# A wavelet convolution and a similarity filter: channel-major partitions, fewer and wider transfers, residual sums in another order

## The chip, the cores and the metric

The kernel runs on one core of a Trainium2 chip. The metric is the device time of one execution in microseconds (us). TensorE (PE) multiplies matrices, VectorE (DVE) and ScalarE (ACT) do elementwise work, GpSimd (POOL) and SyncE (SP) here mostly start DMA transfers, each on a queue of its own.

## The reference

The input x is 8 images of 32 channels, 128 x 128, float32. `_gn` normalises each channel of each image over its pixels. Two layers follow, each with a residual:

```python
x = x + _L0_conv_ref(_gn(x), w0, w1, w2, bias)   # three Haar levels; on each a 5x5 convolution 128 -> 128 channels
x = x + _L1_conv_ref(_gn(x), spatial_weight)

# _L1_conv_ref, K = 5
patches = _extract_patches(x)                             # 25 shifted copies of x
dot = einsum('bchw,bckhw->bkhw', x, patches)
sim = dot / maximum(norm_x[:, None] * norm_p, 1e-8)
weight = (sim + 1.0) * 0.5 * spatial_weight[None, :, None, None]
out = einsum('bckhw,bkhw->bchw', patches, weight)
```

A Haar level splits an image into the four pixels of each 2x2 cell (the quadrants, q = 0 to 3), mixes them, convolves at half size and mixes back. So 32 channels times 4 quadrants fill the 128 partitions.

## The kernel before

Partition 32q + c holds quadrant q of channel c. The first layer convolves image i while the second layer filters image b = i - 1; `iteration(i, ...)` of each engine is one such pair, and the engines meet through counting semaphores, in an order that is written out by hand. Iteration 0 has only the first layer, iterations 1 to 7 have both, and the last has only the second.

An iteration has a head and eight tiles. In the head PE sums the low-pass images and convolves levels 1 and 2, and the first three half-bands of image b are prepared. Tile j (`CONV_TILES` is 8) is point j of a Winograd form of the level-0 convolution (`conv_points`), and between its matmuls, at the places in `HOOKS`, stands the filter work of unit j. A unit is a half-band: 16 rows by 32 columns of each quadrant, with a border, so `UN` = 612 pixels a partition, or `FN` = 720 when it is cut into four overlapping strips.

Half-band h is prepared three tiles ahead of its use (`AHEAD`):
- ACT writes it to st_x2 (`half_in`) and squares it; PE sums the squares over the channels (`norm_piece`, two pieces into stat_ps); ACT takes roots and squared norms (`norms`, into st_a and st_n). Before it writes st_n, ACT waits until the stores of half-band h - 2 have landed (`half_saved`).
- DVE refines the root and makes unit vectors (`units_open`, `units_refine`, `units_close`); ACT and DVE split vectors and values in a high and a low float16 part (st_hl, st_v).
- SP stores all this to HBM (`save_half`): five transfers, to d_hl, d_v (two each) and d_n.
- SP loads it again in another layout (`load_unit`): eleven transfers into unit_mem, that is keys (two), queries (four), values (one) and norms (four, each of 72 rows of 40 bytes). `load_unit(b, u + 2)` stands behind `save_half(b, u + 3)` in SP's queue.

The filter of unit u on PE: `unit_here` waits for the loads; `gram` multiplies keys and queries, DVE turns each product into weights (`weights`, L1012, 128 x 512), `key_values` transposes values, `filter_group` (L1375) multiplies values and weights into out_ps, 32 output columns for each of four row groups g, which are four groups of columns of the array. `residual` (L1364) adds x1 into the same bank: 16 float32 products with 32 columns of a scaled identity as weights, which the hardware runs as 32 instructions. Its loops run over g outside and q inside. ACT writes the result to ostage (`result`), SP to HBM (`store_band`).

POOL's queue loads the raw image twice into `ring`, and reads the outputs of levels 2 and 1 back from HBM into `up`, always in four transfers of 32 partitions, one for each quadrant.

Of the kernel before, what the change touches and what calls it, by code (L numbers as in the profile page):

```python
# [28 lines left out]
P = 128  # L29
# [49 lines left out]
SAVES, LOADS = 80, 176  # L79
# [4 lines left out]
PAD_EDGE = P * (SH + SW - 1)  # L84
# [21 lines left out]
def host_constants():  # L106
# [4 lines left out]
    for c in range(C):  # L111
        for t in range(Q):
            for q in range(Q):
                mix[4 * c + t, C * q + c] = 0.5 * haar[t, q]
                gather[C * q + c, t, C * t + c] = 0.5
    part = np.arange(P)
    average = np.where(part[:, None] % C == part[None] % C, 0.25, 0).astype(np.float32)
    same_quadrant = (part[:, None] // C == part[None] // C).astype(np.float32)
# [37 lines left out]
def build(nc, x, w0, w1, w2, bias, spatial, square, gather, tapmask, unpair, out):  # L156
    ctx = ExitStack()
    with ctx:
# [27 lines left out]
        st_n = sb("st_n", [P, 2, UN], F32)  # L186
# [29 lines left out]
        ones_row = sq_c[0:1, 2, 0:C]  # L216
# [29 lines left out]
        d_n = dram("d_n", [B, 2 * BANDS, Q, UN], F32)  # L246
# [18 lines left out]
        wcomb = sem("wcomb")  # L265
        live_set, live_kept = sem("live_set"), sem("live_kept")
# [93 lines left out]
        def _(sp):  # L360
# [7 lines left out]
            for q in range(Q):  # L368
                sp.dma_start(small[C * q:C * q + C, 6:7], bias.rearrange("(c a) -> c a", a=1)).then_inc(const_in, 16)
# [7 lines left out]
            def save_half(b, h):  # L377

                sp.wait_ge(unit_low, START + 8 * b + h + 1)
                for hl in range(2):  # L380
                    sp.dma_start(d_hl[b, h, hl].rearrange("c q n -> q c n"), st_hl[:, hl, h % 2, :]).then_inc(half_saved[h % 2], 16)  # L381
                for hl in range(2):
                    sp.dma_start(d_v[b, h, hl].rearrange("c q n -> q c n"), st_v[:, hl, h % 2, :]).then_inc(half_saved[h % 2], 16)  # L383
                sp.dma_start(d_n[b, h], st_n[0:P:C, h % 2, :]).then_inc(half_saved[h % 2], 16)

            def load_unit(b, u):
# [19 lines left out]
                norms = d_n[b, u].rearrange("(a q) (h w) -> a (q h) w", a=1, w=SW)  # L406
                for e in range(GROUPS):
                    row = 64 + C * (e // 2)
                    sp.dma_start(norm_strips[s][row:row + 1, e % 2].rearrange("a (n w) -> a n w", w=KW),  # L409
                                 norms[:, :, TW * e:TW * e + KW]).then_inc(unit_in[s], 16)  # L410
# [31 lines left out]
        def _(pool):  # L442
# [5 lines left out]
            def load_raw(batch, c, slot):  # L448
                alone(pool)
                for q in range(Q):  # L450
                    cp = q % 2
                    src = x[batch].rearrange("c (h a) w -> c a h w", a=2)[:, q // 2, CHUNK * c:CHUNK * (c + 1), cp:IMG]
                    dst = ring[C * q:C * q + C, slot, :].rearrange("p (h w) -> p h w", w=IMG)[:, :, 0:IMG - cp]
# [19 lines left out]
            def load_up(i, n):  # L473
# [7 lines left out]
                src = d_z1[i, 2 * C * a:2 * C * (a + 1), BANK * half:BANK * (half + 1)].rearrange("(b c) n -> c b n", c=C)  # L481
                for q in range(Q):
                    pool.dma_start(up[C * q:C * q + C, :].rearrange("c (b n) -> c b n", b=2), src).then_inc(up_in, 16)  # L483

            def iteration(i, nxt, conv, ls):
                if conv:
# [7 lines left out]
                    for q in range(Q):  # L494
                        pool.dma_start(up[C * q:C * q + C, :].rearrange("c (q n) -> c q n", q=Q),
                                       d_z2[i].rearrange("(q c) n -> c q n", c=C)).then_inc(up2_in, 16)
# [27 lines left out]
        def _(act):  # L524
# [98 lines left out]
            def norms(b, h, p):  # L623
# [15 lines left out]
            def count_own(b, h):  # L639
# [3 lines left out]
                nc.scalar.activation(st_hl[:, 1, h % 2, 0:UN], st_n[:, h % 2, :], ACT.Sign, bias=edge[:, :], scale=-1.0,  # L643
# [112 lines left out]
        def _(dve):  # L756
# [17 lines left out]
            def set_live(i):  # L774
# [3 lines left out]
                V.tensor_copy(mean_ls, mean_conv).then_inc(live_set, 1)  # L778
# [168 lines left out]
            def units_open(b, h):  # L947
# [7 lines left out]
                ch.link(dve, V.scalar_tensor_tensor(out=st_b[:, :], in0=st_b[:, :], scalar=-0.5, in1=st_n[:, h % 2, :],  # L955
                                                    op0=ALU.mult, op1=ALU.mult))
# [32 lines left out]
            def set_flag(b, h):  # L989
# [3 lines left out]
                V.tensor_scalar(flag[:, h % FLAGS:h % FLAGS + 1], stat_ps[0:1, 0:1], 0.5, float(P * UN // 2 - pads), ALU.mult, ALU.add)\  # L993
                    .then_inc(flag_done, 1)

            def weights(b, u, k, short_ones):
# [9 lines left out]
                with dve.If(short_ones > 0):  # L1006

                    V.tensor_scalar(dst, guard_ps[0:KN, :].rearrange("p (t n) -> p t n", t=2), 1.0, None, ALU.min)
# [19 lines left out]
            def iteration(i, conv, ls):  # L1028
# [25 lines left out]
                if ls:  # L1054
                    for h in range(AHEAD):
                        units_open(b, h)
                        units_refine(h)
# [15 lines left out]
                for j in range(CONV_TILES):  # L1073
                    h = j + AHEAD
                    if ls:
                        dve.wait_ge(flag_done, START + 8 * b + j + 1)
                        alone(dve)
                        short_ones = dve.value_load(flag[0:1, j % FLAGS:j % FLAGS + 1], min_val=0, max_val=P * UN)
                    for k in range(PAIRS):
                        if ls:  # L1080
# [5 lines left out]
                            if h < 2 * BANDS:  # L1086
# [4 lines left out]
                                if k == 4:  # L1091
                                    units_refine(h)
# [134 lines left out]
        def _(pe):  # L1227
# [124 lines left out]
            def residual(b, u):  # L1352
# [8 lines left out]
                for g in range(BANDS):  # L1361
                    row = BH * r + TH * g
# [180 lines left out]
```

## Time and profile before

| | us |
|---|---|
| median of 3 runs | 2235.41 |
| lowest and highest | 2229.73, 2240.69 |
| the profiled execution, its own time | 2231.01 |
| its span in the trace | 2229.3 |
| PE busy | 1737.3 |
| DVE busy | 1363.9 |
| ACT busy | 742.9 |

The span is the stretch from the first to the last instruction. Busy times of different engines overlap. A granted clock of 1.00 is TensorE's full speed. Iterations 1 to 7 take about 251 to 257 us each and the last some 192 us.

### The profile page before, as it was taken

Reading aid. Unit: us, or ns where it says so; the run is one execution under the profiler, and the core shown is the slowest. Engines: PE = TensorE matmul, PEld = TensorE weight load, DVE = VectorE, ACT = ScalarE, POOL = GpSimd, SP = SyncE. Lnnn points to the kernel's source line nnn. Section 1 sums busy time; section 2 is a strip of 40 time slices with the busy share of each in tenths; the row PEclk is TensorE's granted clock in tenths of the full one; section 3 lists DMA queues with packets and bytes.
Section 4 is the critical chain, followed back from the end, with each engine's and each line's share of the span. In section 5 each row is a group of like instructions: output and inputs, shape, how many; then the busy total and the mean of one; then the engine's idle time right before and its main releaser. Section 6 shows DMA issues by size and latency. Waiting matters only on the chain.

```text
span 2229.3 us, 53057 instructions
## 1 busy us (share of the span) xinstructions
PE 1737.3 (78%) x19007; PEld 988.9 (44%) x19007; DVE 1363.9 (61%) x1995; ACT 742.9 (33%) x1318; POOL 430.6 (19%) x760
## 2 busy tenths in 40 slices
PE   5776887978878787878778787878779787876576
PEld 3542344545444444535345344545345444443354
DVE  6427756756677456856577456755578465865453
ACT  2320243423333243423333243423333252423341
POOL 1343322012311123012310123012300224010000
PEclk7888897889989898989989898999989898987577
DMA  5243337552666337562656447552754447571555
GB/s 164 75 106 95 85 104 174 151 137 78 187 155 159 94 104 191 153 140 78 179 156 151 97 114 196 152 139 79 176 149 128 117 105 201 127 174 38 141 145 127
DMA packets 128073, 296.57 MB, mean 133 GB/s; under 512 B 44532, under 2 KB 77300, under 8 KB 127220
## 3 DMA queue, kind: packets, MB, share of 16 engines
q1 hardware_dynamic: 90864, 190.39, 33.5%
q0 software_dynamic: 36864, 101.47, 17.6%
q8 instruction: 230, 3.77, 0.8%
q14 instruction: 115, 0.94, 0.1%
HBM read 221.92 MB, written 69.83 MB: 131 GB/s over the span
## 4 chain that ended last, share of the span: by engine, by line
PE 41%; DMA 17%; DVE 15%; SPq 13%; issue 10%; ACT 2%; DVEq 1%; POOL 1%; ACTq 0%; POOLq 0%
PE conv L1274 11%; DMA unit_mem<-d_n 8%; DMA d_n<-st_n 8%; PE conv L1248 6%; PE gram L1339 5%; PE out_ps L1364 5%; PE out_ps L1375 3%; SPq L409 3%; PE conv L1233 3%; PE stat_ps L1297 3%; SPq L383 3%; SPq L402 2%; SPq L381 2%; PE vals_ps L1322 2%; PE conv L1484 2%
## 5 line engine op out<-in xcount | busy, mean ns | idle before, releaser
L1012 DVE SCALAR_TENSOR_TENSOR wgt<-gram,tapw 124x512 f32<-124x512 f32 x512 | 350.1, 685 | 476.9 <-PE gram L1339 441.2
L1274 PE MATMUL conv<-thl,wconv 128*128 128x496 f16 (+2 forms) x1920 | 535.5, 407 | 20.0 <-DVE xa L892 10.7
L454 POOL DMA_DIRECT2D ring<-in_x x576 | 334.1, 585 | 666.5 <-ACT xa L526 345.0
L1339 PE MATMUL gram<-unit_mem 128*60 128x128 f16 x4096 | 250.6, 247 | 210.1 <-DMA unit_mem<-d_n 137.9
L1339 PEld LDWEIGHTS gram<-unit_mem 128*60 128x60 f16 x4096 | 152.3, 113 | 420.0 <-issue 419.5
L1274 PEld LDWEIGHTS conv<-thl,wconv 128*128 128x128 f16 x1920 | 167.3, 103 | 215.3 <-issue 62.1
L1248 PE MATMUL conv<-thl,wconv 128*128 128x480 f16 (+7 forms) x1200 | 256.9, 368 | 0.0
L483 POOL DMA_DIRECT2D up<-d_z x128 | 68.5, 537 | 813.1 <-DVE xa L943 755.4
L1297 PE MATMUL stat_ps<-st_sq,sq_c 128*128 128x306 f32 x256 | 117.9, 549 | 125.5 <-DVE flag L993 40.4
L1375 PE MATMUL out_ps<-wgt,vals 124*32 124x128 f32 x4096 | 204.8, 296 | 0.8 <-DVE wgt L1012 0.4
L526 ACT ACTIVATE vals<-vals_ps 124x512 f32<-124x512 f32 x128 | 76.2, 596 | 341.3 <-PE vals_ps L1322 337.6
L526 ACT ACTIVATE thl<-tw 128x1024 f16<-128x1024 f32 x64 | 67.6, 1057 | 339.8 <-DVE tw L828 186.4
L1248 PEld LDWEIGHTS conv<-thl,wconv 128*128 128x128 f16 x1200 | 116.1, 98 | 123.4 <-issue 8.8
L1364 PE MATMUL out_ps<-x,sq_c 128*32 128x128 f32 x2048 | 169.0, 289 | 0.0
L1364 PEld LDWEIGHTS out_ps<-x,sq_c 128*32 128x32 f32 x2048 | 147.9, 115 | 19.9 <-issue 16.2
L526 ACT ACTIVATE st_a<-stat_ps,tiny 128x306 f32<-128x306 f32 x128 | 65.7, 514 | 218.4 <-DMA d_n<-st_n 112.3
L1375 PEld LDWEIGHTS out_ps<-wgt,vals 124*32 124x32 f32 x4096 | 124.3, 115 | 29.3 <-issue 6.4
L526 ACT ACTIVATE ostage<-out_ps,live 128x256 f32<-128x256 f32 x128 | 55.0, 486 | 205.2 <-PE out_ps L1375 205.2
L1297 PEld LDWEIGHTS stat_ps<-st_sq,sq_c 128*128 128x128 f32 x256 | 47.6, 223 | 151.6 <-issue 92.3
L955 DVE SCALAR_TENSOR_TENSOR st_b<-st_b,st_n 128x612 f32<-128x612 f32 x64 | 50.5, 789 | 104.5 <-ACT st_b L526 104.0
L1233 PE MATMUL conv<-xa,gat_c 128*128 128x512 f32 x128 | 79.0, 773 | 35.4 <-issue 19.1
L1322 PE MATMUL vals_ps<-unpair_c,unit_mem 64*60 64x32 f16 x4096 | 89.5, 183 | 1.7 <-issue 1.6
(137 smaller groups left out, 2110.8 us busy)
## 6 DMA issues: line engine op xcount, KB each, us to landing
unit_mem<-d_hl SPq DMA_DIRECT2D x128, 360.0 KB
unit_mem<-d_hl SPq DMA_DIRECT2D x256, 180.0 KB
ring<-in_x POOLq DMA_DIRECT2D x288, 128.0 KB, 3.4
ring<-in_x POOLq DMA_DIRECT2D x288, 127.0 KB, 3.7
d_hl<-st_hl SPq DMA_DIRECT2D x128, 180.0 KB
d_v<-st_v SPq DMA_DIRECT2D x128, 180.0 KB
unit_mem<-d_v SPq DMA_DIRECT2D x64, 360.0 KB
up<-d_z POOLq DMA_DIRECT2D x160, 128.0 KB, 4.9
```

What stands on the lines that cost most here:

```text
L454: pool.dma_start(dst, src).then_inc(raw_in[slot], 16)
L483: pool.dma_start(up[C * q:C * q + C, :].rearrange("c (b n) -> c b n", b=2), src).then_inc(up_in, 16)
L526: return nc.scalar.activation(dst, src, func, bias=bias, scale=scale)
L1012: V.scalar_tensor_tensor(out=dst, in0=g, scalar=SIM_SCALE ** 2, in1=tapw[:, :].unsqueeze(1).to_broadcast([KN, 2, 2 * QN]), op0=ALU.add, op ...
L1233: last = mm(dst, gat_c[:, q, :], src[:, 2 * r0 + q // 2:2 * r1:2, q % 2:2 * side:2], start=(q == 0), stop=(q == Q - 1))
L1248: last = mm(dst[:, a0 - r0:a1 - r0, b0:b1], wconv[:, level - 1, w, t, :], src[:, a0 + dy:a1 + dy, b0 + dx:b1 + dx], start=(n == 0), stop=( ...
L1274: last = mm(dst[:, :, b0:b1], wconv0[:, w, 2 * (p % ROWS4) + s, dx + 2, :], thl[:, p % 2, d, s, :, b0 + dx:b1 + dx] if p % ROWS4 != 1 else ...
L1297: mm(stat_ps[:, 0:PIECE], same_quadrant, st_sq[:, p * PIECE:(p + 1) * PIECE], start=True, stop=True)\
L1322: last = mm(vals_ps[row:row + KQ, C * n:C * n + C], values[s][0:2 * C, q, e, TH * KW * g:TH * KW * g + KQ], unpair_c[:, :], start=True, st ...
L1339: last = mm(bank[row:row + KQ, col:col + QN], key[:, q, e_at, TH * KW * g:TH * KW * g + KQ], tile[:, :, TH * g + 1:TH * g + 1 + TH, 1:1 + ...
L1364: last = mm(o[C * g:C * g + C, q, :].rearrange("p (h w) -> p h w", h=TH), ident[:, C * q:C * q + C], x1[:, row:row + TH, UW * half:UW * (h ...
L1375: last = mm(o[C * g:C * g + C, :, :, TW * e:TW * e + TW], vals[:, (e * BANDS + g) * 2 + c, :], wgt[:, e % 2, g, c * QN:(c + 1) * QN], star ...
```

## The change

The partitions are renumbered: quadrant q of channel c now lies at 4c + q. The constant matrices, the bias and the transfers of `ring` and `up` follow, so each of POOL's transfers now writes 32 partitions that lie 4 apart.

In this order a store's rows stand in HBM in the order of the partitions. `save_half` becomes three transfers: one for both halves of st_hl, one for both halves of st_v (each with 128 partitions outermost, two rows of 1440 bytes a partition), and one for the norms. The norms are written by DVE as strips (st_s, 720 wide, in place of an in-place update of st_n, 612 wide) and stored so that `load_unit` reads them in two transfers of long rows in place of four of 40-byte rows. ACT's count of short vectors (`count_own`) reads the 720-wide strips.

The wait for `half_saved` moves: on ACT from ahead of the norm writes to ahead of the write of st_v, and a second one stands on DVE ahead of the write of st_s in `units_refine`.

`residual` turns its loops about: q outside, g inside, and takes every fourth column of the identity.

The output mean lies on partitions in another order than the filter's output, so once in each iteration four small products of PE reorder it, in tile 7 (`mean_out`).

```diff
-SAVES, LOADS = 80, 176
+SAVES, LOADS = 48, 144
...
-                mix[4 * c + t, C * q + c] = 0.5 * haar[t, q]
-                gather[C * q + c, t, C * t + c] = 0.5
+                mix[4 * c + t, 4 * c + q] = 0.5 * haar[t, q]
+                gather[4 * c + q, t, 4 * c + t] = 0.5
     part = np.arange(P)
-    average = np.where(part[:, None] % C == part[None] % C, 0.25, 0).astype(np.float32)
-    same_quadrant = (part[:, None] // C == part[None] // C).astype(np.float32)
+    average = np.where(part[:, None] // Q == part[None] // Q, 0.25, 0).astype(np.float32)
+    same_quadrant = (part[:, None] % Q == part[None] % Q).astype(np.float32)
...
-        st_n = sb("st_n", [P, 2, UN], F32)
+        st_n, st_s = sb("st_n", [P, UN], F32), sb("st_s", [P, 2, FN], F32)
...
-        ones_row = sq_c[0:1, 2, 0:C]
+        ones_row = sq_c[0:1, 2, 0:P:Q]
...
-        d_n = dram("d_n", [B, 2 * BANDS, Q, UN], F32)
+        d_n = dram("d_n", [B, 2 * BANDS, GROUPS, Q, SN], F32)
...
             def save_half(b, h):
 
                 sp.wait_ge(unit_low, START + 8 * b + h + 1)
-                for hl in range(2):
-                    sp.dma_start(d_hl[b, h, hl].rearrange("c q n -> q c n"), st_hl[:, hl, h % 2, :]).then_inc(half_saved[h % 2], 16)
-                for hl in range(2):
-                    sp.dma_start(d_v[b, h, hl].rearrange("c q n -> q c n"), st_v[:, hl, h % 2, :]).then_inc(half_saved[h % 2], 16)
-                sp.dma_start(d_n[b, h], st_n[0:P:C, h % 2, :]).then_inc(half_saved[h % 2], 16)
+                sp.dma_start(d_hl[b, h].rearrange("l c q n -> (c q) l n"), st_hl[:, :, h % 2, :]).then_inc(half_saved[h % 2], 16)
+                sp.dma_start(d_v[b, h].rearrange("l c q n -> (c q) l n"), st_v[:, :, h % 2, :]).then_inc(half_saved[h % 2], 16)
+                sp.dma_start(d_n[b, h].rearrange("e q n -> q e n"), st_s[0:Q, h % 2, :].rearrange("p (e n) -> p e n", e=GROUPS)).then_inc(half_saved[h % 2], 16)
...
-                norms = d_n[b, u].rearrange("(a q) (h w) -> a (q h) w", a=1, w=SW)
-                for e in range(GROUPS):
-                    row = 64 + C * (e // 2)
-                    sp.dma_start(norm_strips[s][row:row + 1, e % 2].rearrange("a (n w) -> a n w", w=KW),
-                                 norms[:, :, TW * e:TW * e + KW]).then_inc(unit_in[s], 16)
+                for a in range(2):
+                    row = 64 + C * a
+                    sp.dma_start(norm_strips[s][row:row + 1].rearrange("p e (q n) -> p (e q) n", q=Q),
+                                 d_n[b, u, 2 * a:2 * a + 2].rearrange("(p e) q n -> p (e q) n", p=1)).then_inc(unit_in[s], 16)
...
-                    dst = ring[C * q:C * q + C, slot, :].rearrange("p (h w) -> p h w", w=IMG)[:, :, 0:IMG - cp]
+                    dst = ring[q:P:Q, slot, :].rearrange("p (h w) -> p h w", w=IMG)[:, :, 0:IMG - cp]
...
-                src = d_z1[i, 2 * C * a:2 * C * (a + 1), BANK * half:BANK * (half + 1)].rearrange("(b c) n -> c b n", c=C)
+                src = d_z1[i, :, BANK * half:BANK * (half + 1)].rearrange("(c q) n -> c q n", c=C)[:, 2 * a:2 * a + 2]
                 for q in range(Q):
-                    pool.dma_start(up[C * q:C * q + C, :].rearrange("c (b n) -> c b n", b=2), src).then_inc(up_in, 16)
+                    pool.dma_start(up[q:P:Q, :].rearrange("c (b n) -> c b n", b=2), src).then_inc(up_in, 16)
...
-                        pool.dma_start(up[C * q:C * q + C, :].rearrange("c (q n) -> c q n", q=Q),
-                                       d_z2[i].rearrange("(q c) n -> c q n", c=C)).then_inc(up2_in, 16)
+                        pool.dma_start(up[q:P:Q, :].rearrange("c (q n) -> c q n", q=Q),
+                                       d_z2[i].rearrange("(c q) n -> c q n", c=C)).then_inc(up2_in, 16)
...
-                    act.wait_ge(half_saved[h % 2], START + SAVES * (4 * b + h // 2))
                 copy(st_a[:, p * PIECE:(p + 1) * PIECE], stat_ps[:, 0:PIECE], func=ACT.Abs_reciprocal_sqrt,
                      bias=tiny[:, :])
-                copy(st_n[:, h % 2, p * PIECE:(p + 1) * PIECE], stat_ps[:, 0:PIECE]).then_inc(n2_kept, 1)
+                copy(st_n[:, p * PIECE:(p + 1) * PIECE], stat_ps[:, 0:PIECE]).then_inc(n2_kept, 1)
                 if p == 1:
                     act.wait_ge(n2_kept, START + 16 * b + 2 * h + 2)
                     act.wait_ge(unit_low, START + 8 * b + h)
                     copy(st_b[:, :], st_a[:, :], func=ACT.Square).then_inc(root_squared, 1)
+                    act.wait_ge(half_saved[h % 2], START + SAVES * (4 * b + h // 2))
                     copy(in_strips(st_v[:, 0, h % 2, :]), strips(st_x2[:, h % 2, :, :].rearrange("p h w -> p (h w)"))).then_inc(v_high, 1)
...
-                nc.scalar.activation(st_hl[:, 1, h % 2, 0:UN], st_n[:, h % 2, :], ACT.Sign, bias=edge[:, :], scale=-1.0,
+                nc.scalar.activation(st_hl[:, 1, h % 2, :], st_s[:, h % 2, :], ACT.Sign, bias=edge[:, :], scale=-EPS_SIM ** -0.5,
...
-                V.tensor_copy(mean_ls, mean_conv).then_inc(live_set, 1)
+                if first(i):
+                    V.tensor_copy(mean_ls, mean_conv).then_inc(live_set, 1)
+                else:
+                    dve.wait_ge(mean_out, i)
+                    V.tensor_copy(mean_ls, stat_ps[:, 0:1]).then_inc(live_set, 1)
...
-            def units_refine(h):
-                sq = st_n[:, h % 2, :]
+            def units_refine(b, h):
+
                 prep_chain.link(dve, V.scalar_tensor_tensor(out=st_a[:, :], in0=st_b[:, :], scalar=1.5, in1=st_a[:, :],
                                                             op0=ALU.add, op1=ALU.mult))
-                prep_chain.link(dve, V.scalar_tensor_tensor(out=sq, in0=sq, scalar=EPS_SIM ** -0.5, in1=st_a[:, :],
-                                                            op0=ALU.mult, op1=ALU.mult))
+                dve.wait_ge(half_saved[h % 2], START + SAVES * (4 * b + h // 2))
+                prep_chain.link(dve, V.tensor_tensor(in_strips(st_s[:, h % 2, :]), strips(st_n[:, :]), strips(st_a[:, :]), ALU.mult))
 
             def image_of(h):
...
-                for g in range(BANDS):
-                    row = BH * r + TH * g
-                    for q in range(Q):
-                        last = mm(o[C * g:C * g + C, q, :].rearrange("p (h w) -> p h w", h=TH), ident[:, C * q:C * q + C],
+                for q in range(Q):
+                    for g in range(BANDS):
+                        row = BH * r + TH * g
+                        last = mm(o[C * g:C * g + C, q, :].rearrange("p (h w) -> p h w", h=TH), ident[:, q:P:Q],
                                   x1[:, row:row + TH, UW * half:UW * (half + 1)], start=False, stop=False)
                 last.then_inc(res_read, 1)
 
...
+                        if conv_on and j == 2 * BANDS - 1 and k == 7:
+
+                            pe.wait_ge(live_kept, i + 1)
+                            if ls:
+                                pe.wait_ge(n2_kept, START + 16 * b + 16)
+                                pe.wait_ge(flag_done, START + 8 * b + 8)
+                            else:
+                                pe.wait_ge(gn1_var, i + 2)
+                            for g in range(BANDS):
+                                last = mm(stat_ps[C * g:C * g + C, 0:1], average[:, 0:P:Q], mean_conv, start=True, stop=True)
+                            last.then_inc(mean_out, 1)
```

## Rows read from the trace of the kernel before

**Rows 1.** Page, part 1: busy us, share of the span, instructions.
```profile
PE 1737.3 (78%) x19007; PEld 988.9 (44%) x19007; DVE 1363.9 (61%) x1995; ACT 742.9 (33%) x1318; POOL 430.6 (19%) x760
```

**Rows 2.** Windows: busy us of PE, PEld, DVE, ACT, POOL, clock, DMA share, GB/s.
```profile
1271.00:1523.00 252.00, 205.54 (x2386) 114.66 (x2380) 161.67 (x234) 89.06 (x160) 49.14 (x86) 0.93 0.54 140
...
2037.00:2229.00 192.00, 114.97 (x1852) 80.06 (x1852) 86.15 (x141) 65.87 (x121) 0.00 (x0) 0.68 0.49 123
```

**Rows 3.** Page, part 4: the chain that ended last, by engine.
```profile
PE 41%; DMA 17%; DVE 15%; SPq 13%; issue 10%; ACT 2%; DVEq 1%; POOL 1%; ACTq 0%; POOLq 0%
```

**Rows 4.** Waits over the span: waiter, releaser, us in total, times, longest.
```profile
PE gram L1339 <- DMA unit_mem<-d_n: 137.9, 29, 13.5
ACT st_a L526 <- DMA d_n<-st_n: 112.3, 23, 10.1
...
PE stat_ps L1297 <- ACT st_n L526: 37.4, 10, 6.5
```

**Rows 5.** Waits in the last iteration, 2037 to 2229 us.
```profile
PE gram L1339 <- DMA unit_mem<-d_n: 17.7, 6, 6.2
```

**Rows 6.** Timeline of SyncE's queue: start us, us, line, transfer, count.
```profile
1309.76 1.49 SPq L381 DMA_DIRECT2D d_hl<-st_hl  x2
...
1312.89 0.57 SPq L384 DMA_DIRECT2D d_n<-st_n  x1
...
1324.86 3.67 SPq L409 DMA_DIRECT2D unit_mem<-d_n  x4
...
1459.14 1.48 SPq L381 DMA_DIRECT2D d_hl<-st_hl  x2
...
1467.66 4.31 SPq L409 DMA_DIRECT2D unit_mem<-d_n  x4
```

**Rows 7.** Windows of 10 us in that iteration, columns as in Rows 2.
```profile
1311.00:1321.00 10.00, 7.46 (x35) 3.39 (x34) 4.91 (x6) 6.86 (x14) 0.00 (x0) 1.00 0.23 75
1321.00:1331.00 10.00, 9.88 (x48) 4.49 (x46) 5.48 (x8) 5.97 (x11) 0.00 (x0) 1.00 0.85 188
...
1471.00:1481.00 10.00, 3.33 (x40) 1.46 (x39) 3.71 (x5) 2.38 (x3) 5.05 (x9) 0.97 1.04 222
```

**Rows 8.** The chain in order of time: start us, us, what.
```profile
1312.89 7.82 DMA d_n<-st_n
...
1471.24 15.14 DMA unit_mem<-d_n
```

**Rows 9.** Timeline of PE: start us, us, instructions [idle before, releaser].
```profile
1371.77 1.39 PE L1297 MATMUL stat_ps<-st_sq,sq_c 128*128 128x306 f32 x2 [4.24 <-ACT st_n L526]
...
1391.25 0.47 PE L1339 MATMUL gram<-unit_mem 128*60 128x128 f16 x8 [3.74 <-DMA unit_mem<-d_n]
```

**Rows 10.** The same, later in that iteration.
```profile
1486.92 0.64 PE L1339 MATMUL gram<-unit_mem 128*60 128x128 f16 x8 [11.40 <-DMA unit_mem<-d_n]
```

**Rows 11.** Timeline of ACT in the head.
```profile
1320.74 0.52 ACT L526 ACTIVATE st_a<-stat_ps,tiny 128x306 f32<-128x306 f32 x1 [2.45 <-DMA d_n<-st_n]
```

**Rows 12.** Timeline of DVE late in tile 0.
```profile
1367.58 1.21 DVE L882 TENSOR_TENSOR thl<-tw,thl 128x1024 f16<-128x1024 f32 x1
```

**Rows 13.** The chain at tile 0: residual sums, then a whole filter group.
```profile
1348.55 2.06 PE out_ps L1364 x29
...
1353.15 0.57 PE out_ps L1375 x16
```

**Rows 14.** Groups by shape on DVE: count, busy us, mean ns.
```profile
L974 DVE TENSOR_TENSOR st_v<-st_x,st_v 128x720 f16<-128x720 f32 x64 | 57.5, 898 | 0.0
L962 DVE SCALAR_TENSOR_TENSOR st_n<-st_n,st_a 128x612 f32<-128x612 f32 x64 | 50.9, 796 | 2.2
```

**Rows 15.** Groups by shape, weight loads on PE.
```profile
L1484 PEld LDWEIGHTS conv<-sq_c,unit_mem 128*128 128x128 f32 x100 | 24.2, 335 | 11.0 <-issue 10.4 <-ACT xa L526 0.4
...
L1513 PEld LDWEIGHTS gram<-delta,sq_c 128*128 128x128 f32 x12 | 3.4, 316 | 7.8 <-DVE wconv L828 7.4
```

**Rows 16.** Page, part 3: queue, packets, MB, share of 16 engines.
```profile
q0 software_dynamic: 36864, 101.47, 17.6%
```

More of the change, by code:

```diff
@@ L78 @@
 START = 1
-SAVES, LOADS = 80, 176
+SAVES, LOADS = 48, 144
 POINT_MM = 3 * K
 HOOKS = [0, 4, 8, 12, 15, 19, 23, 27, 2 * POINT_MM]
-PAD_EDGE = P * (SH + SW - 1)
+PAD_EDGE = P * (SH + GROUPS * KW - 1)
 PAD_INNER = P * SH
@@ L265, in build @@
         wcomb = sem("wcomb")
+        mean_out = sem("mean_out")
         live_set, live_kept = sem("live_set"), sem("live_kept")
@@ L368, in _ @@
             for q in range(Q):
-                sp.dma_start(small[C * q:C * q + C, 6:7], bias.rearrange("(c a) -> c a", a=1)).then_inc(const_in, 16)
+                sp.dma_start(small[q:P:Q, 6:7], bias.rearrange("(c a) -> c a", a=1)).then_inc(const_in, 16)
             sp.dma_start(spat[:, :], spatial.rearrange("(a k) -> a k", a=1).to_broadcast([P, TAPS])).then_inc(const_in, 16)
@@ L954, in units_open @@
                 dve.wait_ge(root_squared, 8 * b + h + 1)
-                ch.link(dve, V.scalar_tensor_tensor(out=st_b[:, :], in0=st_b[:, :], scalar=-0.5, in1=st_n[:, h % 2, :],
+                ch.link(dve, V.scalar_tensor_tensor(out=st_b[:, :], in0=st_b[:, :], scalar=-0.5, in1=st_n[:, :],
                                                     op0=ALU.mult, op1=ALU.mult))
-            def units_refine(h):
-                sq = st_n[:, h % 2, :]
+            def units_refine(b, h):
                 prep_chain.link(dve, V.scalar_tensor_tensor(out=st_a[:, :], in0=st_b[:, :], scalar=1.5, in1=st_a[:, :],
                                                             op0=ALU.add, op1=ALU.mult))
-                prep_chain.link(dve, V.scalar_tensor_tensor(out=sq, in0=sq, scalar=EPS_SIM ** -0.5, in1=st_a[:, :],
-                                                            op0=ALU.mult, op1=ALU.mult))
+                dve.wait_ge(half_saved[h % 2], START + SAVES * (4 * b + h // 2))
+                prep_chain.link(dve, V.tensor_tensor(in_strips(st_s[:, h % 2, :]), strips(st_n[:, :]), strips(st_a[:, :]), ALU.mult))
             def image_of(h):
@@ L992, in set_flag @@
                 pads = PAD_EDGE if h // 2 in (0, BANDS - 1) else PAD_INNER
-                V.tensor_scalar(flag[:, h % FLAGS:h % FLAGS + 1], stat_ps[0:1, 0:1], 0.5, float(P * UN // 2 - pads), ALU.mult, ALU.add)\
+                V.tensor_scalar(flag[:, h % FLAGS:h % FLAGS + 1], stat_ps[0:1, 0:1], 0.5, float(P * FN // 2 - pads), ALU.mult, ALU.add)\
                     .then_inc(flag_done, 1)
@@ L1006, in weights @@
                 with dve.If(short_ones > 0):
-                    V.tensor_scalar(dst, guard_ps[0:KN, :].rearrange("p (t n) -> p t n", t=2), 1.0, None, ALU.min)
+                    V.tensor_scalar(dst, guard_ps[0:KN, :].rearrange("p (t n) -> p t n", t=2), 1 / EPS_SIM, 1.0, ALU.mult, ALU.min)
                     dve.drain()
@@ L1056, in iteration @@
                         units_open(b, h)
-                        units_refine(h)
+                        units_refine(b, h)
                         units_close(b, h)
@@ L1077, in iteration @@
                         alone(dve)
-                        short_ones = dve.value_load(flag[0:1, j % FLAGS:j % FLAGS + 1], min_val=0, max_val=P * UN)
+                        short_ones = dve.value_load(flag[0:1, j % FLAGS:j % FLAGS + 1], min_val=0, max_val=P * FN)
                     for k in range(PAIRS):
@@ L1091, in iteration @@
                                 if k == 4:
-                                    units_refine(h)
+                                    units_refine(b, h)
                                 if k == 5:
@@ L1437, in hook @@
                                 alone(pe)
-                                short_ones[0] = pe.value_load(flag[0:1, j % FLAGS:j % FLAGS + 1], min_val=0, max_val=P * UN)
+                                short_ones[0] = pe.value_load(flag[0:1, j % FLAGS:j % FLAGS + 1], min_val=0, max_val=P * FN)
                                 unit_here(b, j)
```

## The prediction

> **What bounds the kernel now.** I read the page's busy shares, the chain, the waits, and then one middle iteration (1271 to 1523 us) by windows and by the queues' timelines. PE is busy 78% of the span, DVE 61% [rows 1]; in the middle iteration PE works 205.5 of 252 us at a clock of 0.93, so about 46 us are idle [rows 2]. The chain says whose they are: a sixth of it is DMA and another eighth is SP's queue [rows 3]. Three waits put it in us: `gram` stands 137.9 us for unit_mem, ACT 112.3 us for the stores, and PE another 37.4 us for norms that ACT writes late for that reason [rows 4].
>
> One unit's data go this way: SP starts five stores (1309.76 to 1313.46), which land 7.8 us after the last began, at 1320.7; only then start the eleven loads, which take SP until 1328.53 [rows 6, 8]. While the first stores were alone, the DMA share was 0.23 at 75 GB/s; in the next window, mostly loads, it was 0.85 at 188 [rows 7]. 0.23 is a quarter of 16 engines: a store runs on four of them, at 75 / (0.23 x 16) = 20 GB/s each. The Trainium skill (DMA: Bandwidth & Descriptors, section Why a DMA increments its semaphore by 16 and not by 1) has the rule: a transfer uses the largest number of engines up to 16 that divides the outermost size of both sides. By that rule 128 partitions against four quadrants give four, and the new stores, 128 against 128, sixteen. The trace agrees for the old form (0.23) and has no row for the new one.
>
> That the new form runs on 16 I take from the loads: they have 32 or 64 rows outermost on both sides, and their window shows 0.85.
>
> PE pays at three places in an iteration: 4.24 us for late norms, 3.74 us for unit 2, and 11.40 us for unit 6 [rows 9, 10]. The last is the clearest. 128 x 720 float16 are 180 KB. A half-band's stores are four times that and 9.6 KB, a unit's loads 10 x 180 KB in size, POOL's eight ring and four up transfers at that time 12 x 128 KB. Spread evenly the loads and POOL's put 209 KB on each engine; the stores put 182 KB on each of four. These four carry 391 KB from 1459.14 to 1486.38, when the loads are in [rows 6, 8]: 14.4 GB/s each. So the four engines are the bottleneck.
>
> **The change, part by part**, for each of the seven full iterations.
>
> Stores on 16 engines. 740 KB over 16 is 46 KB an engine, so at unit 6 each has 255 KB to carry; at the same 14.4 GB/s that is 17.7 us, and the loads land near 1477 in place of 1486.4. PE ran dry at 1486.92 - 11.40 = 1475.5 [rows 10]. 1.5 to 2 us of the 11.4 stay: gain 9.4. SP must not be later than the data: it starts the last load at 1472 now [rows 6]. The five stores cost it 3.7 us. A store with 256 rows has no row here; between 0.57 (the small one) and 1.5 (two old ones) I take 1 us each, 2.6 in all. The four norm loads cost 3.67 [rows 6]; two of them lie between 0.6 and 1.8, and I take 1. SP is 3.8 us earlier, so it ends at 1468 and hides. Unit 2: its 3.74 us [rows 9] go, but not all of it need be a gain, since DVE then has its share of the tile left to do: between 0 and 3.74 I take 2.2. The rest of `gram`'s 17 us an iteration (137.9 less 17.7, over seven) [rows 4, 5] stands beside DVE work; I count nothing.
>
> The moved waits. ACT no longer holds the norms for the stores, and the stores land sooner. Of the 4.24 us [rows 9] I take 3, since PE ran dry at 1367.5 and DVE's low part for the next point ended at 1368.8 [rows 12]. In the head ACT stood 2.45 us [rows 11]; gain 1.5. The wait new on DVE comes after both norm pieces and the square of the root, so some 5 us behind the point where ACT waited until 1320.74 [rows 11]. Queued behind it is all of DVE's work, in the tiles the weights of `gram` first, for which PE waits. It costs nothing by that margin, and is the longer covered the sooner the stores land.
>
> Residual sums. They take 2.06 us for 29 instructions, 71 ns each; a filter group soon after takes 0.57 us for 16, 36 ns each [rows 13]. Shapes are alike (32 columns, 128 moving, float32); the filter changes its column group every two instructions, the residual every eight. The new order is the filter's. 32 x 35 ns is 1.1 us a tile. What may spoil it is that the weights are now read with a stride of four columns. Weight loads with a stride of 25 elements took 335 ns beside 316 for close ones, at the start [rows 15]: no more than 6%. The bounds are 0 and 1.1; I take 1.1, and of its 8.8 us an iteration 7, because DVE, with 161.67 us of work in the iteration [rows 2], won't follow at once in every tile. The Trainium skill (TensorEngine Tiling (Array Packing), Theoretical Speedup) gives up to four times for 32 columns. The rows show two times; by the page's figure the sums would fall to 0.6 us and the iteration would gain 5 us more.
>
> What it costs. The strip product on DVE is 720 wide: 898 ns by the nearest row with strips, where 796 ns stood [rows 14]: 8 x 0.1 = 0.8 us, all counted. ACT's count grows alike, off the path. The mean's eight small instructions, at 36 ns up to 71 each [rows 13], are 0.3 to 0.6 us: 0.5. The renumbered constants change no size. POOL's transfers keep count and size, with partitions four apart; no row shows this form. I take no change; a gain would lie in POOL's time, which is off the path, and a loss is the last rival.
>
> Sum: 9.4 + 2.2 + 3 + 1.5 + 7 - 0.8 - 0.5 = 21.8 us, by seven 153. The start and iteration 0 store nothing: 0. In the last iteration `gram` waits 17.7 us [rows 5], of which I take 12, two thirds, as in the others; the residual at a clock of 0.68 [rows 2] is worth 8, earlier stores in its head 4: 24. In all 177 off 2231.0, the profiled execution's own time (span 2229.3): 2054. The median of the runs was 4.4 above it, so 2058; I say 2060.
>
> **The rivals.**
>
> The sums stay serial: consecutive products in other column groups don't overlap when weights are strided, or x1's rows of 32 limit them. Against it stand the filter's 36 ns. The gain falls by 7 x 7 + 8 = 57: 2117.
>
> The waits come back elsewhere. The DMA engines as a whole are already at 1.04 of their share around 1475 [rows 7], and DVE follows PE closely in the tiles. Then the loads gain only SP's 3.8 us once an iteration, the norms nothing: 7 x (3.8 + 7 - 1.3) + 12 = 79, 2156. Against it: outside that window the share is far lower (0.54 mean [rows 2]).
>
> Everything overlaps: the loads never wait (17.2), norms 5.4, head 2.5, residual 13, less 1.3: 37 x 7 + 35 = 293, 1942. It needs DVE to keep up in every tile, which its 162 us of 252 allow only on average.
>
> Slower: POOL's transfers into partitions four apart run at half the rate or less. They use 17.6% of the engines' span, 44 us of an iteration [rows 16], and lie mostly in the same stretches as the loads. Doubling adds 44 us of full DMA load; from about half of it on the path it outweighs the 22 gained. With three quarters on the path the iteration loses 11 us: 2235 + 77 - 24 = 2288. Nothing in the rows speaks for it but that the form is unseen.
>
> **How the numbers follow.** Main case 0.50, range of its own 2010 to 2105 (the gains of tile 6 and the sums a third less, or DVE's share counted as gain too). Serial sums 0.17; waits elsewhere 0.15; everything 0.10, mostly ending between 1950 and 2000; slower 0.05; 0.03 for a gain eaten to within 0.5%, which is about what a measurement of this kernel tells from no change. From 1990 to 2165 all of the first three and a part of the fourth are held, which leaves out some 0.15. Faster 0.92, same 0.03, slower 0.05.
>
> **What would show it.** After the change: a window with stores alone at a share well above 0.5; d_n landing about 4 us after its issue; no wait of `gram` above 3 us at tile 6; ACT's wait for d_n near zero; residual instructions in a third to half the time, about 1.1 us for a tile's; DVE's strip product at 0.9 us; and middle iterations of some 230 us. The prediction is wrong if the store still shows a share of a quarter, if PE's idle time moves from DMA to DVE without getting less, or if ring transfers take longer to land.

## The result and the profile after

The change makes the kernel faster: a median of 2034.36 us (2026.81 to 2041.85, 4 runs) beside 2234.03 us of the kernel before on the same chip. The ratio is 0.910, 95% interval 0.906 to 0.915. Another 5 runs, on another occasion, gave 0.907 (0.903 to 0.912). The prediction was 2060 us, with 2010 to 2105 for the main case.

The page after, part 1 and the engines of part 4 (the chain), answering to [rows 1, 3]:

```profile
PE 1656.1 (81%) x19071; PEld 907.3 (45%) x19071; DVE 1370.9 (67%) x1995; ACT 749.2 (37%) x1318; POOL 426.7 (21%) x760
...
PE 61%; DVE 18%; issue 13%; ACT 4%; DVEq 2%; DMA 1%; POOL 1%; ACTq 0%; SPq 0%; POOLq 0%
```

DMA and SP's queue held 30% of the chain and hold 1%. PE has 81 us less to do, since the residual sums are shorter, and still a larger share of the span, since that is 195 us shorter. The windows of a middle iteration and of the last one, as in [rows 2]:

```profile
1172.00:1400.00 228.00, 194.44 (x2345) 104.37 (x2349) 161.69 (x233) 88.97 (x158) 48.66 (x86) 0.93 0.58 154
...
1860.00:2034.00 174.00, 109.41 (x1852) 72.58 (x1852) 87.91 (x142) 66.89 (x121) 0.00 (x0) 0.65 0.53 137
```

PE's idle time there fell from 46.5 to 33.6 us and its busy time from 205.5 to 194.4. In the waits over the span (waiter, releaser, total, times, longest) no wait of `gram` for its loads is left, nor ACT's for the stores, nor has DVE's new wait for them become one, where [rows 4] have 137.9 and 112.3 us. The longest of PE's waits in total, with the numbers of the kernel after, are now behind DVE:

```profile
PE stat_ps L1299 <- DVE flag L995: 72.7, 38, 3.6
...
PE gram L1341 <- DVE wgt L1014: 39.1, 49, 2.6
```

SP's queue in the head, first half-band (three stores, then the loads), and the window while the stores were alone, answering to [rows 6, 7]:

```profile
1212.41 0.40 SPq L381 DMA_DIRECT2D d_hl<-st_hl  x1
1212.91 0.41 SPq L382 DMA_DIRECT2D d_v<-st_v  x1
1213.51 0.28 SPq L383 DMA_DIRECT2D d_n<-st_s  x1
1216.31 1.19 SPq L398 DMA_DIRECT2D unit_mem<-d_hl  x2
...
1220.22 0.80 SPq L407 DMA_DIRECT2D unit_mem<-d_n  x2
```

```profile
1213.00:1216.00 3.00, 3.00 (x16) 1.37 (x14) 0.93 (x2) 2.61 (x6) 0.00 (x0) 1.00 0.71 250
1214.00:1215.00 1.00, 1.00 (x6) 0.49 (x5) 0.00 (x0) 0.97 (x3) 0.00 (x0) 1.00 1.01 370
```

From the first store to the first load, 11.2 us became 3.9. While the stores are alone the DMA share is 0.71, at 250 GB/s, where it was 0.23 at 75. The 0.71 has the start and the end of the transfers in it; the microsecond in their middle shows 1.01, that is all 16 engines.

A store also costs SP less: 0.40 us for 256 rows. Added up over all 64 half-bands, the stores held SP's queue for 292 us before and hold it for 73. In the kernel before some held it far longer than in the iteration of [rows 6]:

```profile
1862.92 10.93 SPq L383 DMA_DIRECT2D d_v<-st_v  x2
```

The chain at a tile's residual sums, answering to [rows 13], and the new DVE product and the mean's small products in the groups by shape:

```profile
1251.20 1.04 PE out_ps L1366 x32
```

```profile
L965 DVE TENSOR_TENSOR st_s<-st_n,st_a 128x720 f32<-128x720 f32 x64 | 58.1, 908 | 5.3
```

```profile
L1476 PE MATMUL stat_ps<-live,sq_c 128*32 128x1 f32 x64 | 2.0, 185 | 0.0
```

To see where the time came from, one group of matmuls of each iteration serves as a mark: the first 83 of level 2's and level 1's convolution, which stand in the chain as one row. The chain before, first and last of seven, then the chain after:

```profile
279.57 8.96 PE conv L1248 x83
...
1798.92 8.96 PE conv L1248 x83
```

```profile
277.45 8.96 PE conv L1250 x83
...
1650.40 8.96 PE conv L1250 x83
```

Six iterations took 1519.4 us and take 1373.0, that is 253.2 and 228.8 each: 24.4 less. Up to the first mark 2.1 us were gained. From the last mark to the end of the span it was 430.4 and is 384.3: 46.1, of which one more full iteration is 24.4 and the last some 21.7. The prediction had 21.8, 0 and 24.

### The profile page after: what moved, and what is told of

Read it like the earlier page. It is cut to its first block, busy times and chain, and to the rows that moved or that the text cites. A ratio compares the mean times of both kernels' runs of the same rounds, so it can differ in the third digit from the quotient of the medians.

```text
span 2034.7 us, 52625 instructions
## 1 busy us (share of the span) xinstructions
PE 1656.1 (81%) x19071; PEld 907.3 (45%) x19071; DVE 1370.9 (67%) x1995; ACT 749.2 (37%) x1318; POOL 426.7 (21%) x760
## 4 chain that ended last, share of the span: by engine, by line
PE 61%; DVE 18%; issue 13%; ACT 4%; DVEq 2%; DMA 1%; POOL 1%; ACTq 0%; SPq 0%; POOLq 0%
PE conv L1276 16%; PE conv L1250 10%; PE gram L1341 8%; PE out_ps L1377 6%; PE stat_ps L1299 5%; PE conv L1235 5%; PE vals_ps L1324 3%; PE out_ps L1366 3%; DVE wgt L1014 3%; DVE eo L830 2%; PE conv L1497 2%; DVE st_s L965 2%; DVE st_a L962 1%; DVE st_v L976 1%; PE out_ps L1361 1%
## 5 line engine op out<-in xcount | busy, mean ns | idle before, releaser
L1276 PE MATMUL conv<-thl,wconv 128*128 128x496 f16 (+2 forms) x1920 | 529.5, 403 | 41.5 <-issue 15.7
L1341 PE MATMUL gram<-unit_mem 128*60 128x128 f16 x4096 | 253.6, 248 | 65.0 <-DVE wgt L1014 39.1
L1250 PE MATMUL conv<-thl,wconv 128*128 128x480 f16 (+7 forms) x1200 | 265.4, 377 | 0.0
L1299 PE MATMUL stat_ps<-st_sq,sq_c 128*128 128x306 f32 x256 | 114.5, 535 | 115.5 <-DVE flag L995 72.7
L1377 PE MATMUL out_ps<-wgt,vals 124*32 124x128 f32 x4096 | 178.1, 294 | 3.3 <-issue 2.7
L1377 PEld LDWEIGHTS out_ps<-wgt,vals 124*32 124x32 f32 x4096 | 110.4, 116 | 32.1 <-issue 9.8
L1324 PEld LDWEIGHTS vals_ps<-unpair_c,unit_mem 64*60 64x60 f16 x4096 | 78.5, 112 | 47.0 <-issue 46.1
L884 DVE TENSOR_TENSOR thl<-tw,thl 128x1024 f16<-128x1024 f32 x64 | 77.9, 1217 | 10.1 <-ACT thl L524 10.1
```

The costliest lines, as they stand in the source:

```text
L884: V.tensor_tensor(low, tw[:, :], high, ALU.subtract).then_inc(t_ready, 1)
L1250: last = mm(dst[:, a0 - r0:a1 - r0, b0:b1], wconv[:, level - 1, w, t, :], src[:, a0 + dy:a1 + dy, b0 + dx:b1 + dx], start=(n == 0), stop=( ...
L1276: last = mm(dst[:, :, b0:b1], wconv0[:, w, 2 * (p % ROWS4) + s, dx + 2, :], thl[:, p % 2, d, s, :, b0 + dx:b1 + dx] if p % ROWS4 != 1 else ...
L1299: mm(stat_ps[:, 0:PIECE], same_quadrant, st_sq[:, p * PIECE:(p + 1) * PIECE], start=True, stop=True)\
L1324: last = mm(vals_ps[row:row + KQ, C * n:C * n + C], values[s][0:2 * C, q, e, TH * KW * g:TH * KW * g + KQ], unpair_c[:, :], start=True, st ...
L1341: last = mm(bank[row:row + KQ, col:col + QN], key[:, q, e_at, TH * KW * g:TH * KW * g + KQ], tile[:, :, TH * g + 1:TH * g + 1 + TH, 1:1 + ...
```

## The experiments

Each ratio is to the kernel before on the same chip; 1% is 22.4 us. The kernel after stands at 0.907 and 0.910, so I take 0.909 for it. Each takes one part back, unless told otherwise.

**Sums in the old order** (e1_sums_old_order).

```diff
-                for q in range(Q):
-                    for g in range(BANDS):
-                        row = BH * r + TH * g
+                for g in range(BANDS):
+                    row = BH * r + TH * g
+                    for q in range(Q):
```

> The kernel after, with the residual sums back in the old order (row groups outside, quadrants inside), still with weights four columns apart. Theory (the column group must change every two instructions): a tile's 32 instructions go from 1.04 us back to about 2.26 us at full clock, and the time rises by 60 to 85 us, to about 2105. Rival (the weights' stride or another cause made them faster, or their time is hidden beside DVE): instructions stay near 1.04 us, or the time rises by under 20 us.

Ratio 0.938 (0.934 to 0.942): 64 us slower. The chain at a tile's sums has

```profile
1288.73 2.18 PE out_ps L1366 x29
```

so the order alone doubles the time. The weights' stride costs a little in this order: 2.18 us for 29 where [rows 13] have 2.06, or 6%. The weight loads themselves grow by 23%, from 115 ns in the kernel before to 141 in this one, most of which does not show in the sums:

```profile
L1364 PEld LDWEIGHTS out_ps<-x,sq_c 128*32 128x32 f32 x2048 | 147.9, 115 | 19.9 <-issue 16.2
```

```profile
L1366 PEld LDWEIGHTS out_ps<-x,sq_c 128*32 128x32 f32 x2048 | 157.4, 141 | 29.4 <-issue 26.5
```

**The new order alone** (e2_sums_alone), put into the kernel before.

> The kernel before, with nothing changed but the order of the residual's two loops; the weights stay close together. Theory: a tile's sums take 1.1 us, and about 1.1 us a tile are gained where PE and not a DMA is last: 35 to 65 us, ratio 0.97 to 0.985. Rival (the gain of the order shows only when the DMA waits are gone, since the shorter sums only lengthen the next wait for a load): under 20 us.

Ratio 0.979 (0.974 to 0.984): 47 us faster, by 1.01 us for the 32 instructions of a tile:

```profile
1386.44 1.01 PE out_ps L1364 x32
```

This is within what the theory said (35 to 65 us) and above the rival's 20. The same shortening is worth 64 us in the kernel after. The two intervals together are about as wide as the 17 us between them, so that the DMA waits took back a part is likely and not shown. Its `gram` stands 148.7 us for loads, 11 more than before, but two kernels with the same stores and loads (e3 and e9, below) differ by 15 there.

**Stores on four engines** (e3_stores_four). Their HBM side has the four quadrants outermost, as before.

```diff
-                sp.dma_start(d_hl[b, h].rearrange("l c q n -> (c q) l n"), st_hl[:, :, h % 2, :]).then_inc(half_saved[h % 2], 16)
+                for hl in range(2):
+                    sp.dma_start(d_hl[b, h, hl].rearrange("c q n -> q c n"), st_hl[:, hl, h % 2, :]).then_inc(half_saved[h % 2], 16)
```

and the same for d_v.

> The kernel after, with the stores of vectors and values in the old form: four transfers a half-band whose HBM side has the four quadrants outermost. The bytes and rows are the same, but rows land under another channel and quadrant, so the second layer filters shuffled vectors and values. Theory (four DMA engines carried the stores and were what the loads waited for): stores alone show a DMA share near 0.23, gram waits 10 us and more at tile 6 again, and the time rises by 80 to 120 us, to 2115 to 2155. Rival (the gain came from the norm rows and SyncE's shorter issue, or from the ring's partitions): it rises by under 40 us.

Ratio 0.958 (0.953 to 0.963): 110 us slower, more than half of what the whole change brought. The window while stores are alone, and its wait of `gram`:

```profile
1270.00:1278.00 8.00, 5.31 (x26) 2.45 (x24) 5.02 (x6) 5.89 (x12) 0.00 (x0) 1.00 0.26 86
```

```profile
PE gram L1343 <- DMA unit_mem<-d_n: 132.8, 25, 9.0
```

The share is a quarter again, and the wait of [rows 4] is back. SP's queue shows a second effect, two half-bands' stores that are issued while earlier stores, loads and, for the last pair, POOL's `ring` transfers are under way:

```profile
1307.76 3.77 SPq L384 DMA_DIRECT2D d_v<-st_v  x2
1311.72 2.58 SPq L385 DMA_DIRECT2D d_n<-st_s  x1
1319.14 1.35 SPq L382 DMA_DIRECT2D d_hl<-st_hl  x2
1320.59 6.91 SPq L384 DMA_DIRECT2D d_v<-st_v  x2
```

A pair that usually costs 1.35 to 1.5 us takes 6.9 here; in the kernel before one took 10.93. I read it as SP being held while it issues onto engines that are behind; no run separates that from another cause.

**Five stores on 16 engines** (e5_five_stores): the same split in high and low parts, but `"c q n -> (c q) n"` on the HBM side.

> The kernel after, with five stores a half-band in place of three, each with 128 partitions outermost on both sides: high and low parts apart. Theory (the number of engines matters, not the number of transfers): within 10 us of the kernel after, 2034. Rival (fewer transfers and SyncE's issue time matter): SyncE spends some 1.5 us more on each half-band and the time rises by 20 us or more.

Ratio 0.912 (0.908 to 0.915): no difference from the kernel after. Its pairs cost SP 0.90 us, and with its stores alone the share reaches 1.03:

```profile
1220.28 0.90 SPq L382 DMA_DIRECT2D d_hl<-st_hl  x2
1221.27 0.90 SPq L384 DMA_DIRECT2D d_v<-st_v  x2
```

```profile
1222.00:1223.00 1.00, 1.00 (x7) 0.44 (x5) 0.09 (x1) 0.97 (x3) 0.00 (x0) 1.00 1.03 353
```

So the number of engines matters and the number of transfers does not. With e3 this is the pair that decides between the theories: four large transfers each, same bytes and rows of the same length, another order on the HBM side, 5% apart. That the order acts through the number of engines, and not through slower writes to scattered rows, the two windows say: an engine moves 86 / (0.26 x 16) = 21 GB/s while it is busy in e3 and 353 / (1.03 x 16) = 21 in e5.

**ACT's wait early** (e4_wait_early): the wait for `half_saved` ahead of the norm writes.

> The kernel after, with ACT's wait for the stores back at the head of the norm writes; DVE's new wait stays. Theory (with stores that land in 4 us the place of the wait no longer matters, except in the head, where half-band 2 follows half-band 0 closely): within 10 us of the kernel after. Rival (the moved wait is worth the 4 us an iteration that PE stood for norms): 20 to 35 us slower.

Ratio 0.908 (0.904 to 0.912): no difference, as the theory said.

**Norm rows of 40 bytes** (e6_norm_rows): d_n is `[B, 8, Q, UN]`, loaded in four transfers as before.

> The kernel after, with the norms stored in one row of 612 for each quadrant and loaded in four transfers of 72 rows of 40 bytes, as before. The stored norms are those of other pixels; only units with very short vectors read them, and the inputs have none. Theory (load time is hidden now, so 2.7 us more of SyncE's issue and 288 small rows a unit lengthen only the load of unit 6 and those of the last iteration): 5 to 25 us slower. Rival (the small rows were the main cost): 60 us or more slower.

Ratio 0.905 (0.901 to 0.909). Neither theory's loss is there, not even the 5 us of the smaller one; it is within the intervals of the kernel after. Its trace has one wait of `gram` for loads, of 2.3 us: the loads have room for the small rows now.

**Ring into partitions side by side** (e7_ring_blocks).

> The kernel after, with the raw image loaded into 32 partitions side by side, as before, in place of partitions four apart. Channels and quadrants are mixed up by it, in both layers. The ring transfers land 2.7 to 2.8 us after issue in the kernel after and 3.4 to 3.7 in the kernel before. Theory (they landed sooner because the stores freed engines): landing stays under 3.0 and the time within 10 us. Rival (partitions four apart are written faster): landing goes back to 3.4 and more, and the time rises by some us to 30.

Ratio 0.910 (0.906 to 0.914): no difference in time. The issues to `ring` (KB each, median us to landing) in this kernel, then in the kernel after:

```profile
ring<-in_x POOLq DMA_DIRECT2D x288, 128.0 KB, 3.2
ring<-in_x POOLq DMA_DIRECT2D x288, 127.0 KB, 3.3
```

```profile
ring<-in_x POOLq DMA_DIRECT2D x288, 128.0 KB, 2.7
ring<-in_x POOLq DMA_DIRECT2D x288, 127.0 KB, 2.8
```

Here the theory fell: most of the sooner landing belongs to the partitions four apart. It buys nothing that the time shows: DVE waits for the ring 12.3 us in all in this kernel and 5.1 in the kernel after.

**All four parts back** (e8_all_back).

> The kernel after with the four parts taken back together: sums in the old order, stores in four plus one transfers on four engines (rows under other channels and quadrants), norm rows of 40 bytes, ACT's wait early. What stays of the change: the numbering of partitions, POOL's partitions four apart, DVE's strip product and wait, the mean's reordering. Theory: the time of the kernel before within 20 us, 2215 to 2255. Rival (something else of the change brings part of the gain): 2200 or less.

Ratio 1.010 (1.006 to 1.014): the gain is gone, and 1% more, 2264.54 us where the theory ended at 2255. The marks, first and last of seven:

```profile
275.68 8.96 PE conv L1253 x83
...
1814.79 10.56 PE conv L1253 x83
```

This 1%, some 22 us, is what the parts left in place seem to cost, 3.3 us an iteration by the marks (256.5 beside 253.2). Of it DVE's strip product, 0.11 us longer 64 times, could be 7 at most, and the old order's sums with strided weights, 0.12 us longer 64 times, another 8; neither was tried by itself, and the rest is open. But 226 us are more than stores (110) and sums (64) together: 52 were open. Two more kernels divided them, with the kernel after beside them (e12_after_again).

> The kernel after once more, unchanged, beside the next three. Both theories: a ratio near 0.910 to the kernel before. It says whether the 0.905 of the kernel with norm rows of 40 bytes is a gain or the scatter between chips.

Ratio 0.907 (0.903 to 0.912), so the 0.905 of e6 is no gain that can be told from the scatter.

> The kernel after with stores on four engines (rows under other channels and quadrants) and ACT's wait early; norm loads and sums stay new. Stores on four engines alone cost 107 us, with everything else taken back 222, of which the sums are some 63. Theory (the moved wait counts only while stores are slow): ACT waits 80 us and more for d_n again and 20 to 40 us come on top of the four-engine stores, ratio 0.967 to 0.976. Rival (the rest of about 50 us is the norm rows'): under 10 us, ratio below 0.963.

Ratio 0.960 (0.956 to 0.965), 0.958 without the early wait: 5 us, well inside both intervals, where the theory had 20 to 40. ACT does wait 73.7 us for the stores (waits, below), but PE hardly for ACT:

```profile
ACT st_a L526 <- DMA d_n<-st_s: 73.7, 22, 8.8
...
PE stat_ps L1301 <- ACT st_n L526: 5.5, 4, 3.4
```

> The kernel after with stores on four engines (rows under other channels and quadrants) and norm rows of 40 bytes in four loads (norms of other pixels, which only units with very short vectors read); wait and sums stay new. Theory (once loads are waited for, SyncE's 2.7 us more a unit lie on the path): gram's wait for loads rises and 15 to 40 us come on top of the four-engine stores, ratio 0.965 to 0.976. Rival (hidden there too): under 10 us.

Ratio 0.986 (0.980 to 0.992): 62 us on top of e3's 110, more than the 40 at which the theory ended, and `gram` waits 61 us more than e3's 132.8:

```profile
PE gram L1344 <- DMA unit_mem<-d_n: 193.7, 27, 15.0
```

So the small rows cost 62 us while stores run on four engines, and nothing (e6) when they run on 16. Stores 110, norm rows 62 and sums 64 make 236, beside 226 measured. Step by step it is 110, 62 and 54, the last from e10 to e8, for the sums' old order and the early wait together. The marks of e10:

```profile
281.48 10.78 PE conv L1253 x83
...
1777.96 8.96 PE conv L1253 x83
```

**No strip product** (e11_squared_norms). The experiments left DVE and PE as what binds, so the last kernel takes work off DVE. It also loads norm rows of 40 bytes again and waits early on ACT, which e6 and e4 showed to cost nothing with these stores:

```diff
-                prep_chain.link(dve, V.tensor_tensor(in_strips(st_s[:, h % 2, :]), strips(st_n[:, :]), strips(st_a[:, :]), ALU.mult))
...
-                nc.scalar.activation(st_hl[:, 1, h % 2, :], st_s[:, h % 2, :], ACT.Sign, bias=edge[:, :], scale=-EPS_SIM ** -0.5,
+                nc.scalar.activation(st_hl[:, 1, h % 2, 0:UN], st_n[:, h % 2, :], ACT.Sign, bias=edge[:, :], scale=-1 / EPS_SIM,
...
-                sp.dma_start(d_n[b, h].rearrange("e q n -> q e n"), st_s[0:Q, h % 2, :].rearrange("p (e n) -> p e n", e=GROUPS)).then_inc(half_saved[h % 2], 16)
+                sp.dma_start(d_n[b, h], st_n[0:Q, h % 2, :]).then_inc(half_saved[h % 2], 16)
```

> The kernel after without DVE's strip product: ACT's squared norms are stored as they are, in one row of 612 a quadrant, loaded as four times 72 rows of 40 bytes, and short vectors are counted by their squares; ACT waits for the stores at the head of the norm writes. For units with very short vectors, which the inputs don't have, the guard would be the square of what it should be. Theory (stores and loads are hidden, DVE is the next to bind: its strip product is 2% of the chain, 0.9 us a half-band): 15 to 45 us faster than the kernel after, ratio 0.89 to 0.903. Rival (PE alone binds now, or the early wait and small rows give it back): within 10 us of the kernel after.

1991.14 us (1986.5 to 1993.72), ratio 0.889 (0.885 to 0.893): 41 us faster than the kernel after beside it, and the fastest of all. DVE has 59.5 us less to do (page, part 1), and the gain is two thirds of that:

```profile
PE 1638.3 (82%) x19071; PEld 901.0 (45%) x19071; DVE 1311.4 (66%) x1931; ACT 738.9 (37%) x1318; POOL 426.7 (21%) x760
```

That the gain is DVE's saved time is not shown. With the product goes a step of the preparation too, since ACT's count of short vectors stood behind it, for this many us in the kernel after:

```profile
ACT st_hl L641 <- DVE st_s L965: 48.8, 35, 2.4
```

In the new kernel PE waits 61.9 us for DVE's flag in place of 72.7, and `gram` 19.8 us for weights in place of 39.1; PE's own work is 18 us less for the same instructions, at a granted clock of 0.905 in place of 0.897. No run takes these apart.

To be used for any input it needs a square root in the guarded branch, which is entered only where vectors are very short.

## Why the prediction was right

**What bounded the kernel** was read rightly: four DMA engines that carried the stores, with the loads behind them. The 0.23 of [rows 7] became 0.71 and in the middle 1.01, and e3 and e5 differ in nothing but the order of the stores' HBM side. The Trainium skill's rule (DMA: Bandwidth & Descriptors, section Why a DMA increments its semaphore by 16 and not by 1) holds in all forms tried: 4 outermost against 128 gave 0.23 and 0.26, 128 against 128 gave 1.01 and 1.03.

**The sum against the marks.** From the kernel after to e10 an iteration grows by 20.6 us (249.4 less 228.8): stores on four engines and small norm rows. The prediction had 16.1 for these and the moved wait together. From e10 to e8 it grows by 7.1, the sums and the early wait; the sums were booked at 7. What e8 keeps of the change costs 3.3, booked at 1.3. So 24.4 in place of 21.8 is 4.5 too little for the stores and loads, 0.1 for the sums and 2.0 too little for the costs, and that the last took back nearly half of the first is luck. Each figure is from one profile; kernels of equal time (the kernel after, e4, e5, e7, e12) stand between 228.1 and 229.8 an iteration.

**Stores and loads** were the term that was sized too small. The prediction left 1.5 to 2 us at tile 6 and gave no value to the waits beside DVE work; after the change no wait for loads remains, of 17 an iteration. It also took SP's five stores at 3.7 us from the one iteration that it read and the new ones at 2.6; over all half-bands they mean 4.6 and 1.1. The 740 KB of a half-band's stores are 730 by the sizes it gives, which changes nothing.

**Parts are not additive**, and here the prediction was silent. It booked the norm rows as SyncE's issue time, hidden behind the data. Where the stores are slow they cost 62 us; where they are fast, nothing. Which of the two it is, SyncE's 2.9 us more for each load or the 288 small rows on engines already behind, the runs don't separate.

**The moved wait** was booked, with the sooner landing, at 3 and 1.5 us an iteration. Its place makes no difference with stores on 16 engines (e4) and none that can be seen with four (e9). PE's waits for norms that ACT wrote late were 37.4 us [rows 4]; they are 5.5 in e9, 22.1 in e8, where the small rows and the old sums stand too, and are missing in e4 and e10. So stores on four engines do not make the 4.24 us of [rows 9] alone, and with 16 it is gone wherever the wait stands.

**Residual sums**: 57 us in all were booked. Taken back they cost 64, added to the kernel before they bring 47. In e1 the marks

```profile
276.18 10.54 PE conv L1250 x83
...
1700.11 8.96 PE conv L1250 x83
```

give 237.3 us an iteration, 8.5 more than the kernel after. The row that decided was the filter's 36 ns; the new form runs at 1.04 / 32 = 33 ns. The up to fourfold speed of the Trainium skill (TensorEngine Tiling (Array Packing), section Theoretical Speedup) did not come; a little over twice did (71 to 33 ns), as the rows had it. That strided weights cost no more than 6% came true for the sums by chance: the 6% was read from weight loads of another shape, and these weight loads grew by 23%.

**The costs**: the strip product took 908 ns where 898 were taken, the mean's eight instructions 2.0 us of busy time in all eight iterations. What else makes them 3.3 us an iteration is open. And DVE's product was priced by its growth alone, 0.1 us; that all of it might go, and 41 us with it, was not seen.

**The rivals**: serial sums fell by e1. Slower POOL transfers fell by e7, which shows the opposite. That everything overlaps wanted 37 us an iteration and 24.4 came, with 33.6 us of PE idle left. Waits elsewhere may hold in a small part: PE's norm sums wait 72.7 us for DVE's flag, 40.4 in the kernel before, so some 32 us of the DMA waits look to have turned into waits for DVE; PE's idle time still fell by 12.9 us an iteration.

## What to carry to other kernels

A low DMA share beside a long landing (0.23 and 7.8 us here) is a sign that a transfer runs on few engines: look at the outermost dimension on both sides, and choose the layout so that the partitions are outermost in HBM too. Price small rows and extra transfers by whether the loads are waited for at all, since the same rows cost 62 us in one kernel and nothing in another. Where products use 32 columns of the array, let the column group change from one product to the next (33 ns an instruction in place of 71). And read a queue over the whole run, not in one iteration: a pair of stores took 1.34 us in the one that was read and 10.93 in another.

## What the runs showed of the hardware that was not expected

- SyncE's issue time falls with the number of engines: two stores of 128 rows took 1.49 us on four engines [rows 6] and 0.90 on 16 (e5), and one of 256 rows on 16 took 0.40.
- Transfers of 128 KB by POOL into 32 partitions four apart landed 2.7 us after issue, into 32 side by side 3.2 (e7). In e3, with the slow stores, they landed after 2.8, so it is not the stores. The transfers to `up` landed after 4.9 us before, 2.7 after and 3.0 in e3.
- Weight loads of 32 float32 columns took 115 ns close together and 141 with a stride of four. They made serial sums 6% longer (2.18 us for 29 against 2.06), and alternating ones 3% (1.04 us for 32 against 1.01 in e2).
